# Q of the last token block by seven half-size products in place of eight

## The reference

```
n  = layernorm(x)
Q  = n @ Wq.T            # 32 heads of 128, in 8 groups of 4 heads
K, V = ctx @ Wk.T, ctx @ Wv.T   # 8 heads of 128, one for each group
p  = softmax(causal(Q K^T / sqrt(128)))     # inside each batch of 64 tokens
x  = x + tanh(g_xattn) * ((p V) @ Wd.T)
x  = x + tanh(g_ffn) * (layernorm(x) @ dequantised(qweight).T + bias)
```

## Time and profile before

| | before |
|---|---|
| median of three runs | 1057.8 us |
| profiled execution, its own time | 1056.85 us |
| its span on the core | 1054.9 us |
| TensorE busy | 1017.7 us (96%), 7842 matmuls |
| VectorE busy | 682.1 us (65%) |
| ScalarE busy | 456.6 us (43%) |
| GpSimd busy | 233.9 us (22%) |
| mean granted clock of TensorE | 0.995 |
| HBM read / written | 94.11 MB / 25.17 MB |

### The profile page before, as it was taken

The page is one execution under the profiler, slowest core; times in us unless marked ns, Lnnn a source line. Parts: engine busy times, 40 slices in busy tenths (PEclk is TensorE's granted clock), DMA queues, the critical chain, the costliest instruction groups (busy, mean ns, idle before and its releaser), DMA issues.

```text
span 1054.9 us, 19976 instructions
## 1 busy us (share of the span) xinstructions
PE 1017.7 (96%) x7842; PEld 569.2 (54%) x7842; DVE 682.1 (65%) x1374; ACT 456.6 (43%) x917; POOL 233.9 (22%) x245
## 2 busy tenths in 40 slices
PE   5889999999999999999999999999999999999995
PEld 3455555555555555555555554555555555555542
DVE  6856677777577666765466556755556664555678
ACT  5767676676533243333334333244433322333322
POOL 1355565465604000210002100210000300000013
PEclk9999999999999999999999999999999999999998
DMA  7757645445355632345422743333432443224111
GB/s 278 235 153 272 216 163 182 161 135 157 102 178 196 149 90 66 141 133 137 132 71 70 206 134 121 109 119 93 131 122 108 133 137 126 62 86 143 64 36 60
DMA packets 90219, 142.61 MB, mean 135 GB/s; under 512 B 31248, under 2 KB 64016, under 8 KB 79504
## 3 DMA queue, kind: packets, MB, share of 16 engines
q1 hardware_dynamic: 90128, 141.34, 42.0%
HBM read 94.11 MB, written 25.17 MB: 113 GB/s over the span
## 4 chain that ended last, share of the span: by engine, by line
PE 87%; DVE 7%; ACT 3%; issue 2%; DMA 1%; SPq 0%; DVEq 0%; ACTq 0%
PE pa L1295 42%; PE py L1295 30%; PE av L1408 5%; PE pp L1391 3%; PE ps L1375 2%; PE py L1466 2%; PE pp L1375 2%; DVE q L897 1%; DVE sc L943 1%; DMA raw_q<-in_wqT 1%; DVE sc L954 1%; DVE row_max L941 1%; DVE sc L937 1%; ACT q L677 1%; PE av L1442 0%
## 5 line engine op out<-in xcount | busy, mean ns | idle before, releaser
L1295 PE MATMUL pa<-xT,wq 128*128 128x512 f16 x1536 | 342.7, 379 | 9.5 <-DVE q L897 6.7
L1295 PE MATMUL py<-wd,att 128*128 128x512 f16 x1488 | 336.2, 379 | 0.8 <-issue 0.8
L1295 PEld LDWEIGHTS pa<-xT,wq 128*128 128x128 f16 x1536 | 145.8, 98 | 189.9 <-issue 22.5
L1295 PEld LDWEIGHTS py<-wd,att 128*128 128x128 f16 x1488 | 143.3, 98 | 159.1 <-issue 1.1
L677 ACT ACTIVATE q<-pa 128x512 f16<-128x512 f32 x128 | 75.7, 591 | 264.3 <-PE pa L1295 264.3
L976 DVE SCALAR_TENSOR_TENSOR xacc<-py,f_y,xacc 128x512 f32<-128x512 f32 x128 | 95.7, 747 | 125.0 <-PE py L1295 124.9
L728 ACT ACTIVATE att<-av 128x256 f16<-128x256 f32 x256 | 80.8, 384 | 145.7 <-PE av L1408 145.2
L967 DVE SCALAR_TENSOR_TENSOR att<-av,att 128x256 f16<-128x256 f32 x256 | 93.3, 416 | 67.1 <-ACT att L728 66.9
L897 DVE SCALAR_TENSOR_TENSOR q<-pa,q 128x512 f16<-128x512 f32 x128 | 87.7, 685 | 57.0 <-ACT q L677 54.2
L1295 PE MATMUL pa<-wv,cT 128*128 128x128 f16 x1536 | 96.2, 219 | 0.0
L1295 PEld LDWEIGHTS pa<-wv,cT 128*128 128x128 f16 x1536 | 89.9, 98 | 0.9
(11 more groups left out here) (131 smaller groups left out, 1060.1 us busy)
## 6 DMA issues: line engine op xcount, KB each, us to landing
wq<-kept_q SPq DMA_DIRECT2D x24, 1024.0 KB, 7.1
wd<-kept_d SPq DMA_DIRECT2D x23, 1024.0 KB, 4.8
v_dup<-v_nat SPq DMA_DIRECT2D x128, 128.0 KB, 2.4
raw_d<-in_wdT SPq DMA_DIRECT2D x8, 1024.0 KB, 10.1
kept_q<-wq SPq DMA_DIRECT2D x8, 1024.0 KB, 8.8
kept_d<-wd SPq DMA_DIRECT2D x8, 1024.0 KB, 5.4
raw_q<-in_wqT SPq DMA_DIRECT2D x7, 1024.0 KB, 5.6
wk<-kept_k SPq DMA_DIRECT2D x24, 256.0 KB, 7.3
```

Of the source, the lines that this page charges most:

```text
L1295: last = pe.matmul(out, stationary(a, i), moving(b, i), start=(i == 0 and (a, b) == PASSES[0]), stop=(i == count - 1 and (a, b) == PASSES[ ...
```

## The change

Only the last block's Q (m = 24 to 31, `fast(m)`) is made in another way. For a pair r of heads (0, 1 or 2, 3) the product of [2 heads x 512] by [512 x 512 tokens] is seen as a 2 x 2 product of halves: the weight halves A11, A12 (head even, contraction half 0 and 1), A21, A22 (head odd) and the data halves B11, B21 (tokens 0 to 255), B12, B22 (tokens 256 to 511). Seven half products replace eight, by sums and differences of the A's and of the B's. Each half product (`run(m, r, i)`) is 2 contraction chunks x 3 passes = 6 matmuls of 256 columns.

- The weight sums (4 per pair, for all 8 groups) are made in eight steps, n = 13 to 20 (`mixing(n)`): SyncE loads the raw Wq (`load_mix`, 1 MB), GpSimd makes four sums or differences of 512 elements (`mix_weights`, after K of step n + 1 is split), ScalarE and VectorE split them into high and low (`mix_hi`, `mix_lo`, four instructions each), and SyncE writes them to memory (`keep_mix`, 1 MB). In the last block they are loaded again (`back_mix`, 1 MB a step).
- The data sums of block 3 are made in step 20 (`mix_norm`, four GpSimd instructions; `mixed_hi` on ScalarE, `mixed_lo` on GpSimd) and go through 32 more DMA transposes in steps 21 and 22, while 8 of the 32 plain ones fall away. The layernorm of blocks 2 and 3 moves one step earlier (`norm_step` gives 3 in place of 4).
- In a fast step the seven products of a pair pass through one bank half each (X, Y, Z) with four intermediate values: ScalarE copies three of them out of PSUM (`copy_p1`, `copy_p5`, `copy_u2`), VectorE adds three of them back (`add_11`, `add_22`, `add_12`), and then four quadrants are split (`hi_..`, `lo_..`, 256 elements each, in place of two heads of 512). Later products are added on top of a bank whose earlier content has been copied, so they wait for that copy.
- `y_unit(n - 1, 2)` and `y_unit(n - 1, 3)` are moved from the end of a step into the Q of the next (`deferred`), and Wd is loaded after the second of them.
- To make room in SBUF the sums share memory with raw weights that are no longer in use, and the linear layer uses `xs` in place of `xn`. `ffn_zero` of the last tiles goes to one place in step 25.

TensorE's order in a fast step and the waits of a run:

```diff
+                if fast(m):
+                    run(m, 0, 1)
+                    run(m, 0, 5)
+                    run(m, 0, 2)
+                    run(m, 0, 6)
+                    y_unit(n - 1, 2)
+                    run(m, 0, 7)
+                    run(m, 0, 3)
+                    run(m, 1, 1)
+                    run(m, 0, 4)
+                    run(m, 1, 5)
+                    run(m, 1, 2)
+                    run(m, 1, 6)
+                    y_unit(n - 1, 3)
+                    run(m, 1, 7)
+                    run(m, 1, 3)
+                    p_transpose(n, 0)
+                    run(m, 1, 4)
...
+                elif (r, i) == (1, 5):
+                    pe.wait_ge(c12_ok, pair_count(m, 0))
+                elif (r, i) == (1, 2):
+                    pe.wait_ge(c11_ok, pair_count(m, 0))
+                elif i == 6:
+                    pe.wait_ge(p1_ok, pair_count(m, r))
+                elif i == 7:
+                    pe.wait_ge(u2_ok, pair_count(m, r))
+                elif i == 3:
+                    pe.wait_ge(p5_ok, pair_count(m, r))
+                elif i == 4:
+                    pe.wait_ge(c22_ok, pair_count(m, r))
...
+                for kc in range(2):
+                    for c, d in PASSES:
+                        first = kc == 0 and (c, d) == PASSES[0]
+                        last = pe.matmul(half(bank), a[:, c, head, w_half + kc, :], b[:, d, b_half + kc, at],
```

ScalarE and VectorE in a fast step, up to K:

```diff
+                if fast(m):
+                    copy_p1(m, 0)
+                    exp(n, 0)
+                    copy_p5(m, 0)
+                    copy_u2(m, 0)
+                    exp(n, 1)
+                    hi_11(m, 0)
+                    p_part(n, 0)
+                    hi_22(m, 0)
+                    hi_12(m, 0)
+                    copy_p1(m, 1)
+                    hi_21(m, 0)
+                    p_part(n, 1)
+                    copy_p5(m, 1)
+                    copy_u2(m, 1)
+                    hi_11(m, 1)
+                    hi_22(m, 1)
+                    hi_12(m, 1)
+                    p_transposed(n, 0)
+                    hi_21(m, 1)
...
+                if fast(m):
+                    scores(n, 0)
+                    scores(n, 1)
+                    add_11(m, 0)
+                    normalise(n, 0)
+                    add_22(m, 0)
+                    add_12(m, 0)
+                    lo_11(m, 0)
+                    lo_22(m, 0)
+                    lo_12(m, 0)
+                    normalise(n, 1)
+                    lo_21(m, 0)
+                    p_part(n, 0)
+                    y_late(2)
+                    p_part(n, 1)
+                    add_11(m, 1)
+                    y_late(3)
+                    add_22(m, 1)
+                    add_12(m, 1)
+                    lo_11(m, 1)
+                    lo_22(m, 1)
+                    lo_12(m, 1)
+                    lo_21(m, 1)
...
+                    k_part(m)
+                    if g == 1 and tb == BLOCKS - 1:
+                        for t in LATE:
+                            ffn_zero(t)
```

The sums of the weights on GpSimd, and SyncE's queue:

```diff
+            def mix_weights(g):
+
+                pool.wait_ge(s_ld, 16 * (g + 1))
...
+                pool.tensor_tensor(a22, a22, a21, ALU.add).then_inc(s_mix, 1)
+                pool.tensor_tensor(a21, a11, a21, ALU.subtract).then_inc(s_mix, 1)
+                pool.wait_ge(s_mix, 4 * g + 2)
+                pool.tensor_tensor(a11, a22, a11, ALU.subtract).then_inc(s_mix, 1)
+                pool.wait_ge(s_mix, 4 * g + 3)
+                pool.tensor_tensor(a12, a12, a11, ALU.subtract).then_inc(s_mix, 1)
...
+                if fast(m + 1):
+                    back_mix(m + 1)
+                transpose_first(n)
+                if fast(m) and n < LAST:
+                    back_d(n)
+                transpose_rest(n)
                 if m < STEPS:
                     duplicate_v(m)
...
+                if mixing(n) is not None:
+                    keep_mix(mixing(n))
+                if mixing(n + 1) is not None:
+                    load_mix(mixing(n + 1))
```

More of the change, by code:

```diff
@@ L26 @@
 STEPS = BLOCKS * GROUPS
+HB = BT // 2
+HK = D // 2
 HI, LO = 0, 1
@@ L443, in _ @@
                     back_d_last()
-                if GROUPS <= n < LAST:
+                if GROUPS <= n < LAST and not fast(m):
                     back_d(n)
@@ L568, in _ @@
                     split_wv(1)
+                if mix_of(n) is not None:
+                    mix_norm(mix_of(n))
                 if call is not None:
                     ln_rstd(call)
+                if ffn_of(n) is not None and fast(n + 1):
+                    for t in range(ffn_of(n) * TILES, (ffn_of(n) + 1) * TILES):
+                        ffn_add(t)
                 if tb == 0:
@@ L573, in _ @@
                         split_wd(g, h)
+                if mixing(n) is not None:
+                    pool.wait_ge(k_lo, n + 2)
+                    mix_weights(mixing(n))
+                if mix_of(n) is not None:
+                    for t in range(TILES):
+                        mixed_lo(mix_of(n), t)
                 if call is not None:
@@ L579, in _ @@
                         residual(t)
-                if ffn_of(n) is not None:
+                if ffn_of(n) is not None and not fast(n + 1):
                     for t in range(ffn_of(n) * TILES, (ffn_of(n) + 1) * TILES):
@@ L809, in _ @@
                 av_part(n, 2)
+                if mixing(n) is not None:
+                    mix_hi(mixing(n), (0, 1))
                 if prep:
@@ L813, in _ @@
                 av_part(n, 3)
+                if mixing(n) is not None:
+                    mix_hi(mixing(n), (2, 3))
                 if prep:
@@ L821, in _ @@
                     ctx_squares(tb + 1, squares_done(g + 2) + 2 if tb == 0 else squares_done(GROUPS))
+                if mix_of(n) is not None:
+                    for t in range(TILES):
+                        mixed_hi(mix_of(n), t)
                 if call is not None:
@@ new lines, in _ @@
+                if fast(m):
[21 more added lines that the diff above has]
+                    lo_21(m, 1)
+                    if ffn is not None:
+                        ffn_scaled(t0)
+                    k_part(m)
+                    if g == 1 and tb == BLOCKS - 1:
+                        for t in LATE:
+                            ffn_zero(t)
+                    if ffn is not None:
+                        ffn_scaled(t0 + 1)
+                        ffn_scaled(t0 + 2)
+                    if call is not None and g == 0:
+                        ln_stats(call)
+                    av_part(n, 0)
+                    av_part(n, 1)
+                    if ffn is not None:
+                        ffn_scaled(t0 + 3)
+                    v_part(m)
+                else:
+                    scores(n, 0)
+                    if n == 0:
+                        for h in range(2, HPG):
+                            split_wq(1, h)
+                    q_part(m, 0)
+                    scores(n, 1)
+                    normalise(n, 0)
+                    q_part(m, 1)
+                    if n == 0:
+                        weight_scale(1, slice(3, 4))
+                        step_factors(n)
+                    if ffn is not None:
+                        ffn_scaled(t0)
+                    p_part(n, 0)
+                    normalise(n, 1)
+                    q_part(m, 2)
+                    if ffn is not None:
+                        ffn_scaled(t0 + 1)
+                    p_part(n, 1)
+                    q_part(m, 3)
+                    if ffn is not None:
+                        ffn_scaled(t0 + 2)
+                        ffn_scaled(t0 + 3)
+                    k_part(m)
+                    if call is not None and g == 0:
+                        ln_stats(call)
+                    av_part(n, 0)
+                    av_part(n, 1)
+                    v_part(m)
```

456 lines of the change are left out of this document (358 added, 98 removed).

## The result

| | before | after |
|---|---|---|
| median | 1057.98 us (6 runs beside it) | 1068.7 us (6 runs, 1067.09 to 1071.49) |
| span of the profiled execution | 1054.9 us | 1065.4 us |
| matmuls | 7842 | 8130 |
| HBM read / written | 94.11 / 25.17 MB | 110.89 / 33.55 MB |

The account below looks back on a forecast made before the run. TensorE's instruction stream was taken as the bound. Span 1054.9 - 11.3 saved + 2.9 waits = 1046.5 us; adding 2.9 from profiled span to median gives 1049.5 us, own range 1047 to 1052.5, overall 1046 to 1056.

Parts of the forecast that it names:

- R1: Rival, fast steps: dearer hand-offs or 256-element evictions make run (1,4) and neighbours wait 0.5 us a step, 1053.5 us; chance 0.17.
- R2: Rival, fast steps: every new eviction costs like a whole head's, so add_22 comes late; 1060 us; chance 0.12.
- R4: Rival, Q in fast steps: price per matmul, not per column, +1.2 us a step at 0.140 us each, 1070 us; chance 0.02.
- R5: Rival, last block: the change does not take effect in the eight steps, so no change, 1058 us; chance 0.03.
- (d): Step 16: GpSimd starts its four sums only after ln_rstd, so ScalarE is late and y3 waits 1.15 us.
- (c): Step 25: four ffn_zero stand before the p V low parts, so y0 waits 0.85 us.
- (a): Step 24: two more VectorE statistics at y2 and y3 make add_22 late, a wait of 0.2 us.
- (b): Step 25: ScalarE's four layernorm high parts from step 24 delay the first p1 copy; run (0,6) waits 0.55 us.
- (e): Step 9: two more VectorE statistics exceed its idle time, a wait of 0.15 us.
- What I cost at nothing: Steps 13 to 22 and Wd loads: other weight sums, VectorE low parts, SyncE loads and transposes are covered; no added time.
- Do the runs wait?: Fast-step layout, 256-element evictions at 0.39 and 0.40 us: no waits, 28.87 us against 30.27, smallest margin 0.4 us at (1,4).
- R3: Rival, all eight preparation steps: late Wd or late sums cost 0.6 us each, as in step 16; 1054 us; chance 0.06.

Follow-up runs that it names:

- the full queue: Sums spread, stores late, residual and ffn_zero moved; against that kernel, 24 plain transposes put in step 20, data sums' 16 and 16 in steps 21, 22: 1047.84 us.
- the quiet run: The changed kernel with GpSimd's ln_lo, residual and ffn_add of steps 16, 17 and 19 cut from 512 to 8 columns: 1058.11 us.
- the preparation alone: The changed kernel with steps 12 to 21 kept, but Q of every block made by the old products: 1065.57 us, ratio 1.0069 to the kernel before.

## Why the prediction was wrong

**Right: the saving.** 28.87 us for a fast step was forecast and measured; in step 26 six matmuls of 256 columns start every 0.655 us and run (1,4) waits nowhere, and VectorE is 2.2 us busier (18.92 for 16.73 in most steps before; 2.7 had been forecast). The gain is 8 x 1.41 = 11.3 us. With it R1 (a thinner chain), R2 (evictions at full-head prices), R4 (a price per matmul) and R5 fall. R2 ended on the right side and still was not the cause: it put the loss in every fast step, and there is none.

**Right or near: four of the five single waits.** (d) in step 16 is 1.19 us for 1.15; (c) in step 25 is 0.93 for 0.85; (a) 0.33 for 0.2; (b) 0.18 of waiting (0.34 by pitch) for 0.55. The chain of (d) came as laid out: GpSimd's sums start behind `ln_rstd`, at 1.26 to 1.33 us each. (e) did not come in step 9; 0.3 us more came in step 12 (below).

**Wrong: "What I cost at nothing".** That one step failed, in two sentences of it. The forecast had 2.9 us of waits in all; 18.9 us more came, the span being 1065.4 for 1046.5.

First sentence: "steps 21 and 22 have 20, 27 us, so V's copies are issued as late as S + 33 and are needed at S + 47". I looked at one step's queue and at one transfer behind the transposes. V's copies were indeed in time (they went out at S + 37.4 and S + 40.5, and no wait is theirs). I did not ask when the transposes themselves are needed (the last of them by run (0,4), S + 8.5 of step 23, where S comes 5.2 us earlier since two y units left step 22), nor when the queue gets to them, which three steps' contents decide. Most of the sum was to be had: 56 transposes x 1.33 = 75 us. Loads, `keep_mix` and V's copies between them take 14 us in the queue after (696.36 to 785.61 less the transposes), and 1.2 us pass from the last transpose to the run: 90 us from the first one. Run (0,4) wants them 30.27 + 30.27 + 25.09 + 8.5 = 94.1 us after S of step 20. So the first must go out by S + 4. It went out at S + 16.4, behind the stores and `keep_mix`, 12.4 too late; 4.76 of it step 20's own loss hides, and the rest, 7.6, is the wait (7.9). With the full queue it goes at S + 2.4 (679.81), and the wait is 0.7, since the other transfers take 16 us there. Cost 10.66 us: 7.9 of waiting and 2.8 of clock, which the forecast had at nothing.

Second sentence: "VectorE's 2.8 us of low parts push the next scores to S + 2.9 at worst". That is 0.69 us for each part, a price from rows beside which GpSimd was quiet. In steps 16 and 19 the preparation puts VectorE's instructions with two SBUF operands beside GpSimd's, and both get dearer. The prediction knew it ("VectorE and GpSimd disturb each other in places") and used it for R1 alone. With GpSimd quiet the scores start at S + 3.1, so the count of instructions was right and the price was not. Cost: 3.9 us in step 20 and 1.17 in step 17. The last 0.9 in step 20 goes against the other half of the sentence, "by the earlier trace rows 3.1 was still free": in those rows GpSimd is quiet. In step 20 it makes the data sums while VectorE shifts and normalises the scores, and with the scores at S + 3.1 TensorE waited 0.94. That is read from the rows of the quiet run, not from a run without the data sums. The trace of before had such a row, VectorE's 256 elements in 0.60 us beside GpSimd in step 25, 0.42 elsewhere:

```profile
829.20 5.12 POOL L550 TENSOR_TENSOR xacc<-xacc,ff_rows 128x512 f32<-128x512 f32 x4
...
830.14 0.60 DVE L943 TENSOR_TENSOR sc<-sc,row_max 128x256 f32<-128x256 f32 x1
```

**Step 25** lost 2.96 us for 1.40. Here the slowed instructions are those of the fast step itself, for which "Do the runs wait?" took 0.40 us each. VectorE and GpSimd:

```profile
848.71 2.89 DVE L1194 SCALAR_TENSOR_TENSOR q<-junk,q 128x256 f16<-128x256 f32 x2
...
879.56 0.76 DVE L1194 SCALAR_TENSOR_TENSOR q<-junk,q 128x256 f16<-128x256 f32 x2
```

```profile
845.76 5.55 POOL L732 TENSOR_TENSOR xacc<-xacc,ff_rows 128x512 f32<-128x512 f32 x4
```

In step 25 the pair stands beside GpSimd's `residual` and takes 2.89 us, in step 26 it takes 0.76. Normalise(1) is late by that, ScalarE's copies of (1) stand behind the cast that waits for it, and run (1,7) waits 1.17 us (1.33 by pitch). Moving `residual` and `ffn_zero` away took 2.6 of the 2.96 us back.

R3 came nearest in kind, costs in the preparation steps, but gave them 0.6 us each from late weight sums and Wd; no run shows a wait for Wd.

What stays open: the 0.3 us of step 12, which also stands in the run without any sums, and which step 20 has there too. There the fourth head of Q waits 0.37 us for VectorE, whose L1451 takes up to 1.42 us for 0.74, and L1290 1.00 for 0.69, beside GpSimd. The likely reason is the layernorm, which the change moves one step earlier and with it GpSimd's low parts, but no run moves it back. Open is also why a wait of a few us is followed by the lower clock in some places and not in others (below).

## What to carry to other kernels

For every transfer that a change adds, write down when its first reader wants it and when the in-order queue can have issued it, over all the steps that the queue is busy without a gap, and look for what holds the queue's head. A duration is a row's only beside what ran with it: where a change puts new VectorE work with two SBUF operands beside GpSimd, price it from such a row, or keep the two apart. And when two halves of a change measured alone add up to nothing while the whole loses, the loss is at a place where one half hands over to the other.

## What the runs showed of the hardware that was not expected

The slowdown goes by the kind of instruction and its operands. Beside a busy GpSimd, 512 elements from two SBUF tensors take 1.6 us (L1194 on `raw_d`) or 1.48 (L1290) in place of 0.7, while those with one operand in PSUM keep their time (L1323, 0.74 to 0.75 us; L1314 0.74 to 0.76 a pair). With one SBUF tensor both are found: L1288 (TENSOR_REDUCE) keeps its 0.69 us (587.03, beside GpSimd's L732), but the layernorm's L1400 (TENSOR_SCALAR) takes 3.64 for four beside GpSimd's sums (573.09), 1.91 elsewhere (837.57). The side effect is mutual: GpSimd's instruction of that shape goes from 1.26 us (570.30 in step 16) to 1.6 (6.47 / 4).

The clock after a wait: 7.9, 4.7, 4.6, 4.1 and 3.4 us of waiting in step 23 (five kernels) were each followed by some 5 us at a granted 0.50 to 0.53, 0.7 us by none. But a 3.0 us wait in step 20 was followed by 0.61 over 4.4 us in the change and by 1.00 with the preparation alone, where the step has the same 35.0 us: there VectorE sets its end either way, and the lost clock only took the place of a second wait of 1.6 us.
